# Row-sum reciprocals written repeated and spread by two whole transposes

## The reference

```
x = layernorm(x + attention0(x))   # rmsnorm, 16 heads of 64, softmax over 256 keys
x = layernorm(x + moe0(x))         # 8 experts (top 2) and a shared one, 256 wide, gelu
x = layernorm(x + attention1(x))   # 16 heads of 8, attending over the heads of one token
x = layernorm(x + moe1(x))         # 8 experts (top 2), 512 wide, gelu
```

## Time and profile before

| what | value |
|---|---|
| runs, median (lowest to highest) | 1565.22 us (1562.77 to 1567.48) |
| the profiled execution, its own time | 1567.07 us |
| its span in the profile | 1565.3 us |
| instructions | 34497 |
| granted TensorE clock, mean | 0.976 |

### The profile page before, as it was taken

The page is one execution under the profiler, slowest core; times in us unless marked ns, Lnnn a source line. Parts: engine busy times, 40 slices in busy tenths (PEclk is TensorE's granted clock), DMA queues, the critical chain, the costliest instruction groups (busy, mean ns, idle before and its releaser), DMA issues.

```text
span 1565.3 us, 34497 instructions
## 1 busy us (share of the span) xinstructions
PE 1421.9 (91%) x12096; PEld 1249.4 (80%) x12096; DVE 985.5 (63%) x2534; ACT 860.9 (55%) x2361; POOL 514.5 (33%) x415
## 2 busy tenths in 40 slices
PE   6897999999999999999999999999999999998847
PEld 5675888888888888878888888888888887887747
DVE  4456576675757667575666757667575766757482
ACT  5564655656465564647556464655646465463403
POOL 3206061340605134060522506043250614315040
PEclk9898999999999999999999999999999999998978
DMA  7000000000000000000000000000000000000000
GB/s 239 4 2 1 5 2 8 0 7 0 0 7 0 7 0 7 0 0 7 0 7 0 7 0 0 7 0 7 0 1 5 0 7 0 3 1 1 4 1 7
DMA packets 14088, 13.78 MB, mean 9 GB/s; under 512 B 1625, under 2 KB 12770, under 8 KB 13794
## 3 DMA queue, kind: packets, MB, share of 16 engines
q1 hardware_dynamic: 14050, 13.27, 2.6%
HBM read 11.17 MB, written 2.10 MB: 8 GB/s over the span
## 4 chain that ended last, share of the span: by engine, by line
issue 62%; POOL 17%; POOLq 14%; PE 4%; DVE 1%; ACT 1%; DMA 0%; DVEq 0%; SPq 0%
POOLq L329 8%; POOL hid L466 6%; POOL hid L471 6%; POOLq L473 5%; POOL std_inv L427 2%; PE bank_F L1101 1%; POOL up_lo L436 1%; POOL x L488 1%; POOL x_plus L450 1%; POOL rms_inv L443 1%; PE bank_S L983 0%; DMA b_out<-in_b_out 0%; ACT probs L544 0%; DVE hid L743 0%; DVE hid L761 0%
## 5 line engine op out<-in xcount | busy, mean ns | idle before, releaser
L1101 PE MATMUL bank_F<-down,hid 128*128 128x128 f32 x3072 | 374.9, 278 | 34.6 <-DVE x L731 34.0
L1101 PEld LDWEIGHTS bank_F<-down,hid 128*128 128x128 f32 x3072 | 359.4, 193 | 46.3 <-DVE x L731 38.1
L544 ACT ACTIVATE probs<-bank_S,neg_max 128x256 f32<-128x256 f32 x512 | 235.5, 475 | 179.0 <-DVE neg_max L652 178.9
L652 DVE TENSOR_REDUCE neg_max<-bank_S 128x2 f32<-128x512 f32 x256 | 164.6, 684 | 83.5 <-PE bank_S L983 80.2
L471 POOL TENSOR_TENSOR hid<-hid,qkv 128x1024 f32<-128x1024 f32 x62 | 177.1, 2857 | 47.1 <-ACT hid L560 47.1
L731 DVE SCALAR_TENSOR_TENSOR x<-bank_F,gates,x 128x128 f32<-128x128 f32 x512 | 155.2, 345 | 31.6 <-PE bank_F L1101 21.4
L523 ACT ACTIVATE probsT<-bank_T 128x512 f32<-128x512 f32 x256 | 139.6, 605 | 44.1 <-PE bank_T L1012 44.0
L426 POOL TENSOR_TENSOR var_eps<-mv,ln_eps 128x2 f32<-128x2 f32 x64 | 12.5, 195 | 428.5 <-DVE mv L690 428.5
L441 POOL TENSOR_TENSOR mean_sq<-sum_sq,one_over_d 128x2 f32<-128x2 f32 x16 | 3.1, 194 | 455.1 <-ACT h_row L518 455.1
L1012 PE MATMUL bank_T<-ident,probs 128*128 128x128 f32 x1024 | 138.4, 279 | 0.1
L459 POOL TENSOR_TENSOR hid<-qkv 128x1024 f32<-128x1024 f32 x47 | 112.2, 2386 | 66.6 <-ACT qkv L523 66.6
(11 more groups left out here) (167 smaller groups left out, 3259.1 us busy)
## 6 DMA issues: line engine op xcount, KB each, us to landing
x_row<-in_x SPq DMA_DIRECT2D x16, 128.0 KB, 2.1
down<-in_w SPq DMA_DIRECT2D x1, 2048.0 KB, 14.0
out<-x SPq DMA_DIRECT2D x16, 128.0 KB, 1.8
hid<-in_w SPq DMA_DIRECT2D x1, 1536.0 KB, 7.8
hid<-in_rw SPq DMA_DIRECT2D x1, 1024.0 KB, 6.6
hid<-in_wv SPq DMA_DIRECT2D x1, 512.0 KB, 3.8
hid<-in_wq SPq DMA_DIRECT2D x1, 512.0 KB, 4.7
hid<-in_wk SPq DMA_DIRECT2D x1, 512.0 KB, 5.6
```

Of the source, the lines that this page charges most:

```text
L544: ins = sc.activation(probs[:, h // 2 % 2, h % 2, t, :], unit.bank(f"S{h}")[:, t * S:(t + 1) * S], ACT.Exp, bias=neg_max[:, h, t:t + 1], a ...
L652: ve.tensor_reduce(neg_max[:, h, :], v.bank(f"S{h}")[:, :].rearrange("p (t k) -> p t k", t=NT), AX.X, ALU.max, negate=True).then_inc(max_r ...
L1101: ins = te.matmul(bank[:, (j * NT + t) * P:(j * NT + t + 1) * P], hid[:, e, k, tokens(t)], down[:, e, k, :], start=k == 0, stop=k == m - 1)
```

## The change

Three edits.

1. `row_inv` grows from 2 x 4 to 2 x 2 x 2 x 64 values per partition. VectorE's reciprocal reads each of the four sums 64 times and writes 256 values.
2. TensorE's four products a step become two whole transposes, one for each token tile: 128 columns, 64 of each head.
3. `x2` becomes another name for `x1`, and `ao` for `h_row`. VectorE gets one wait more, for `x2plus_ready`, before the residual of `OUT` is written to `x1`.

```diff
-        row_inv = sb("row_inv", P, 2, 2 * NT)
+        row_inv = sb("row_inv", P, 2, NT, 2, DH)
...
-        x2 = sb("x2", P, NT, D)
+        x2 = x1
...
-        ao = sb("ao", P, NT, NH1, DH1)
+        ao = h_row[:].rearrange("p t (h d) -> p t h d", h=NH1)
...
-                settled(dve, ve.reciprocal(row_inv[:, s % 2, :], row_sum[:, s % 2, :]).then_inc(inverse_ready, 1))
+                sums = row_sum[:, s % 2].rearrange("p (j t a) -> p t j a", j=2, a=1)
+                settled(dve, ve.reciprocal(row_inv[:, s % 2], sums.broadcast_to([P, NT, 2, DH])).then_inc(inverse_ready, 1))
...
                     dve.wait_ge(xplus_ready, v.at(0, 1, 1))
+                    if v.b:
+                        dve.wait_ge(x2plus_ready, v.at(1, 1, 1))
                     residual(v, "OUT", x1, x_plus)
...
                     for t in range(NT):
-                        for j in range(2):
-                            n = j * NT + t
-                            te.matmul(bank[j * DH:j * DH + DH, S + t * P:S + (t + 1) * P],
-                                      row_inv[:, s % 2, n:n + 1].broadcast_to([P, DH]), ident[:], start=True, stop=True)
+                        te.transpose(bank[:, S + t * P:S + (t + 1) * P], row_inv[:, s % 2, t].rearrange("p j e -> p (j e)"), ident[:])
...
-                    return transpose_row(bank, ao[:].rearrange("p t h d -> p t (h d)"))
+                    return transpose_row(bank, h_row)
```

## The result

The changed kernel took 1715.07 us (1713.76 to 1717.6, 4 runs) beside 1564.06 us (1562.77 to 1567.48) for the kernel before on the same chip: a ratio of 1.0964, 95% interval 1.0941 to 1.0987. It is slower by 151 us. The forecast was 1683 us, with a range of 1645 to 1745.

A forecast was written before the change was run, and what follows sets the result against it. The prediction took VectorE's reciprocal, straight before head_max, to set the attention steps. Profiled 1567.1 us, plus 110 for lateness, plus 8 for TensorE's clock, less 1.9 to the runs' median, gave 1683 us; range 1645 to 1745.

The forecast's parts named there:

- What bounds: Attention steps: VectorE's reciprocal stands straight before head_max, which releases ScalarE and TensorE's next scores; the o_scale wait moves along.
- The third rival: Attention steps: the 14.1 us added fit into VectorE's 16.5 us of idle, time stays at 1565 us; chance 0.06.
- The price of the reciprocal: VectorE: 256 elements take 1.93 us, 1.76 us more than now, 8 times an iteration.
- The low end of the bounds: Reciprocal on VectorE: with all 166 ns of the 2-element one fixed, 6.2 ns an element and 1.74 us.
- the central value: Reciprocal on VectorE: line through the 4- and 16-element sizes, 7.0 ns an element plus 141 ns fixed, 1.93 us.
- The steeper rival: Reciprocal on VectorE: a floor hides a slope of 8.5 ns, price 2.29 us, kernel 1723 us; chance 0.2.
- streaming: Rival on VectorE: the reciprocal runs like any instruction at 0.42 us, kernel 1547 us; chance 0.06.
- TensorE's part: Two transposes for four products save 0.27 us a step, at most 35 us, counting for nothing when steps are late.
- The walk: One iteration followed by head_max lateness, less what idle absorbs: 6.9 us an iteration, 110 us over 16.
- The clock: TensorE's gaps in steps 5 and 6 bring half clock: 0.5 us an iteration, 8 us.
- the fourth rival: TensorE falls to half clock in every iteration, 3 us in place of 0.5, kernel 1723 us; chance 0.13.
- Moved buffers: x2 as x1, ao in h_row: no cost, the added wait before OUT's residual being over some 27 us before.

The follow-up runs named there:

- e8: Changed kernel, but VectorE's reciprocal is of 4 elements and a two-operand VectorE instruction (maximum of the value and itself) spreads it to 256, in the same place: 1616.35 us.
- e9: e8 with the reciprocal and the spreading instruction moved between lower_qk and o_scale: 1574.11 us, ratio 1.0061 to the kernel before.
- e5: Changed kernel with the wide reciprocal moved from in front of head_max to between lower_qk and o_scale, same instructions: 1665.05 us.
- e12: e8 with the spreading written as a tensor_reduce over an axis of length one, the four reciprocals also written in another order: 1589.37 us.
- e11: e9 with the spreading written as a tensor_reduce, so e12's instructions moved between lower_qk and o_scale: 1570.05 us, ratio 1.0024 to the kernel before.
- e2: Changed kernel, but TensorE spreads the 256 written reciprocals by the four old products in place of the two transposes: 1716.53 us.
- e7: Changed kernel with TensorE's projections of head pair 4 computed twice, needless instructions in the gap before D0p3: 1696.7 us.
- e13: e10 with the edit of e7 added (projections of head pair 4 computed twice): 1648.92 us, ratio 1.052 to the kernel before.
- e1: Kernel before with only the third edit, the moved buffers and the wait for x2plus_ready: 1563.84 us, ratio 0.9998.
- e10: Changed kernel with the two h_row instructions of step 3 moved ahead of the wide reciprocal of the same step: 1657.41 us.

## Why the prediction held, point by point

**What bounds.** Right. The wide reciprocal stands in front of `head_max`, and the `o_scale` wait did not shrink with it (93.1 us). Moving the same instructions (e8 to e9, 42 us; changed kernel to e5, 50 us; e12 to e11, 19 us with no hold on what was moved) shows that place, not the sum of busy time, sets the cost. The third rival, all hidden, fell.

**The price of the reciprocal.** Mis-sized: 1.93 us forecast, 1.742 measured. The three sizes 2, 16 and 256 lie on one line: 87 ns over 14 elements and 1489 ns over 240 are both 6.2 ns an element. The low end of the bounds was right, and the 169 ns of the 4-element one, on which the central value rested, was the odd one. The steeper rival fell, and so did streaming. By the reading made of the Trainium skill, "VectorE: DVE Perf Modes", section "Walkthrough: the 8-slice pipeline in each mode", the slope was 8.3 ns; the measurement decides for 6.2. Its direction, many cycles an element, was right.

**TensorE's part.** Mis-sized, without effect: 0.12 us a step saved in place of 0.27, worth nothing in e2.

**How much shows.** The walk gave 1.2, 0.7, 0.7, 1.7, 2.5, 4.3, 6.1 and 6.9 us. Taken without the half clock and the hold of `h_row`, that is e7's lateness less 1.7 us from step 4 on, the runs gave 1.2, 0.9, 0.9, 1.9, 2.4, 3.8, 5.4 and 7.0. The sum is right by luck, by two errors that cancel: the price was 0.19 us too high in each step, and 1.0 us was counted as given back at the last reciprocal and never came. Its wait of 1.57 us stayed 1.57. ScalarE's copies were not long done: they are queued behind the exponential of attention1 (L560), which waits for VectorE (L767) just in front of the late `head_max`. That nothing is given back in the up products was right (10.2 us late at 765.84 and at 797.08). That all 16 iterations lose alike was not: they lose 0.7 to some 13 us, and why the second one loses most was not followed up.

**The clock.** Mis-sized: 0.5 us an iteration forecast, 1.5 measured (e7), half of the 3 us of the fourth rival. The cost came not in steps 5 and 6, where it was looked for. The clock falls there too, in front of `head_max` of step 5 and behind that of step 6:

```profile
742.00:744.00 2.00, 2.00 (x12) 2.00 (x12) 1.97 (x2) 1.46 (x4) 1.86 (x3) 0.52 0.00 0
...
760.00:762.00 2.00, 2.00 (x11) 2.00 (x11) 1.91 (x2) 0.07 (x1) 2.00 (x2) 0.50 0.00 0
```

But VectorE is busy there up to the `head_max` at 747.57 and the `o_scale` at 765.84, neither of which waits. The cost came in step 2, where `head_max` waits for TensorE (1.89 us at 722.40) and the walk kept the lateness at 0.7: TensorE's D0p3 is between the late mix and the scores. That was right about the order and left out the clock.

**Missed.** GpSimd's hold of `h_row`, 1.7 us an iteration. A late VectorE instruction met a GpSimd one that it had been ahead of by 0.6 us. The Trainium skill, "SBUF — State Buffer", section "Who interferes with whom", states it: VectorE and GpSimd share one port pair as an exclusive lock, instructions with two SBUF inputs or in a two-port mode wait for it, and a `tensor_reduce` never does. Every run here agrees: copies, `tensor_scalar` and two-input instructions were held (2.43, 2.07 and 2.55 us), reductions (0.420 us) and reciprocals (1.742 us) not once.

**The account of one iteration.** 10.2 us = 7.0 for the reciprocals, 1.5 for the half clock, 1.7 for the hold of `h_row`. The 7.0 is what is left when the two measured terms are taken off. e13 closes it from the other side: 97.14 us, which is 92.17 plus 7.0 less the 2.0 us that VectorE's product is no longer held, a hold that the kernel before has too. The forecast was 6.9, 0.5 and nothing. The 2.8 us between, over the twelve full iterations, are 33 us, next to the 32 by which 1683 fell short. The other four iterations together lose some 5 us less than forecast, and some 4 us lie in the executions compared: the medians differ by 151 us, the two profiled spans by 147. So the measured 1715 us lies in the range, but the width of the range was argued from a steeper reciprocal and a slower clock, and more than half of what was missing came from a hold that the prediction does not have.

**Moved buffers.** Right: nothing (e1).

## What to carry to other kernels

Look at where an instruction stands before its length: an engine that is idle a third of the time can still pass every added microsecond on, if the idle time waits for a chain that starts with that engine. Divide before you spread: a reciprocal's cost here goes by the elements it writes. When an edit makes an engine late, look up what the late instructions will now run beside (GpSimd's products here) and which TensorE groups come behind the longer gap, and price both.

## What the hardware showed that was not expected

- A reciprocal costs 6.2 ns an element of float32 with some 154 ns fixed (2, 16 and 256 elements: 166, 253, 1742 ns); a reduction that writes 256 elements takes 420 ns.
- VectorE's copies, scalar products and two-input instructions from SBUF wait out a running GpSimd instruction (0.29 us becomes 2.4 us); the reverse holds too, GpSimd's sum of 1.27 us took 2.07.
- TensorE's standstill of 1.73 us was followed by half clock, and those of 1.32 (kernel before) and 1.04 us (e7) were not. In e10 the standstill is 1.73 us in all 13 iterations too, and half clock followed in 6 of them only, so the gap alone does not settle it. What does stays open.
- What stays open: the 2.0 us for which VectorE's product is held in the kernel before as well. e10 shows that it can be had by order. The kernel before with that order was not run, and no version run beat it.
